# Wide attention: one reciprocal per four steps, spread to rows by DMA, multiplied by GpSimd a pass later; the output of two head pairs accumulates in PSUM

## The chip, the cores and the metric

The kernel runs on one core of one Trainium2 chip. The metric is the device time of one execution, in microseconds. The median of three runs before the change is 1040.21 us (1037.43 to 1385.11). One execution was taken by the profiler, and the trace rows below are all of that one.

## The reference

Eight sublayers in a row (four attentions, four feed-forward blocks) act on x of 4 batches x 256 tokens x 128 features, each added through a tanh gate. The change touches two of them, the "wide" attentions L1 and L3: 16 heads of 64 features, 256 queries and 256 keys per batch. Apart from names, for each batch and head:

```python
q, k, v = x @ Wq, ctx @ Wk, ctx @ Wv          # 1024 wide, 16 heads of 64
# L1 (first call):  scores masked, then w = relu(scores * scale + nbias) ** 2
# L3 (second call): scores clipped to -11..11, then w = exp(scores * scale)
attn = w / w.sum(-1)                          # L1 adds 1e-32 to the sum
out  = concat_heads(attn @ v) @ Wo            # (256, 128) per batch (+ bo in L3)
```

The division by the sum is done late: the kernel multiplies the 64 x 256 result of `w @ v` by the reciprocal of the sum.

## The kernel before

Every engine has its own instruction stream, written by hand in program order, with waits on counting semaphores between the engines. There is no scheduler: the order of the calls in each engine's `body` is the order on the engine.

A wide attention (`wide_pe`, `wide_act`, `wide_pool`, `wide_dve`; call `c` is 0 for L1 and 1 for L3) makes four **passes** (`NQ`), each over four heads, that is two **head pairs**. A pass has eight **steps** g: a step is one head pair (g // 4) and one batch (g % 4). Two steps make a **slot** k = g // 2: one head pair for one half of the 1024 tokens. The first three passes ran in a hardware loop (`Fori`), the last was written out. The work of a step and who does it:

- `scores(g)`, TensorE: twelve 64-row products into PSUM banks 0-1 or 2-3, two steps ahead of their use.
- `bound(g)`, VectorE: clips or masks the 128 x 1024 scores into one of three buffers `w_p`. It waits until GpSimd has read what stood there (`ps`).
- `weights(g)`, ScalarE: Square or Exp on that buffer.
- `values(g)`, TensorE: the weights times v, into bank 4 (two steps side by side).
- `add(g)`, GpSimd: adds the two key halves into one of two buffers `w_ps`, for the sums. It waits until `denominators` has read the last contents (`dn`).

Once per slot:

- `denominators(k)`, TensorE: sums over the keys, into bank 5, each sum repeated on 32 rows (row block 32 x (2 x head + batch)).
- `reciprocal(k)`, VectorE, on 128 x 256 (in call 0 with an addition of 1e-32 ahead of it).
- `spread(k)`, TensorE: multiplies the reciprocals by a 0/1 matrix so that each of the 64 rows of a head has them, into bank 5.
- `sums(k)`, ScalarE: copies bank 4 to SBUF (`w_pv`); `normalise(k)`, VectorE: `w_pv` times bank 5, into `w_at`.
- `output(k)`, TensorE: `w_at` times Wo, into bank 6; `add(k)`, VectorE: adds bank 6 to the accumulator `xn`.
- `project(k)`, TensorE: q and k of a slot two ahead, into banks 6 and 7; `high` (ScalarE) and `low` (VectorE) split them into two fp32r parts. `wide_values` (TensorE, four tiles per pass, banks 6 and 7) and `value_tiles` (ScalarE) make v of the next pass; `wide_weights` (VectorE, once per pass) splits the next pass's weights.

Banks 6 and 7 are thus shared by `project`, `wide_values` and `output`, and bank 5 by sums and spread reciprocals. Line numbers of before that the rows use: L180 to L182 are the three products of `mm3` (`project`, `wide_values`), L678 `scores`, L691 `values`, L704 `denominators`, L711 `spread`, L719 `output`, L811 `weights`, L851 GpSimd's `add`, L867 and L869 `wide_weights`, L896 `bound` of call 1, L905 `reciprocal` of call 1, L910 `normalise`, L917 VectorE's `add`.

## Time and profile before

| | us |
|---|---|
| median of three runs | 1040.21 |
| the profiled execution | 1033.27 |
| its span | 1031.5 |
| TensorE busy | 844.6 (82% of the span) |
| VectorE busy | 749.3 (73%) |
| ScalarE busy | 446.5 (43%) |
| GpSimd busy | 164.2 (16%) |

The span is what the trace covers; the profiled execution took 1.8 us more. Shares of busy time are averages over eight different sublayers. What the change is worth is read in the two stretches of the wide attentions: the first call from 239.4 us to 397.5 us, the second from 690.9 us to 839.1 us (from the first `values` product to the end of the last `add`).

### The profile page before, as it was taken

What the parts mean: (1) busy time and instruction counts of PE and PEld (TensorE: products, weight loads), DVE (VectorE), ACT (ScalarE), POOL (GpSimd) and SP (SyncE); (2) the same over time, 40 slices, a digit from 0 to 9 for tenths busy, and PEclk for the clock granted to TensorE, in tenths of its full rate; (3) what the DMA queues carried; (4) which work ended last, traced back from release to release, by engine and by line L of the source; (5) the groups of instructions that cost most, each with busy time, mean ns of one, the idle gap of its engine ahead of it and who ended that gap; (6) DMA issues with size and microseconds to landing.
All of it is one profiled execution on the core that took longest, in us unless ns stands there. A gap on an engine that the chain in (4) does not pass through costs nothing. (4 is left out here: it accounts for less than half of the span.)

```text
span 1031.5 us, 14938 instructions
## 1 busy us (share of the span) xinstructions
PE 844.6 (82%) x5066; PEld 602.6 (58%) x5066; DVE 749.3 (73%) x1370; ACT 446.5 (43%) x662; POOL 164.2 (16%) x131
## 2 busy tenths in 40 slices
PE   2688877768889898999947888469899958999996
PEld 2555545445656567677725554346666636777774
DVE  4688765767677776588766887758768675878785
ACT  2254452114344441599912454134443423555553
POOL 1000010003122221022220000113313220111112
PEclk9699999999989997799956999679999987999998
DMA  8000000040000000000200060000000000000000
GB/s 339 1 1 0 1 1 0 0 163 1 1 0 0 0 2 1 0 1 0 83 0 1 0 260 2 0 1 1 1 0 0 1 1 1 1 0 0 0 1 21
DMA packets 1916, 22.78 MB, mean 22 GB/s; under 512 B 209, under 2 KB 209, under 8 KB 1105
## 3 DMA queue, kind: packets, MB, share of 16 engines
q1 hardware_dynamic: 1872, 22.22, 5.3%
q8 instruction: 25, 0.41, 0.2%
q14 instruction: 19, 0.15, 0.0%
HBM read 21.70 MB, written 0.52 MB: 22 GB/s over the span
## 5 line engine op out<-in xcount | busy, mean ns | idle before, releaser
L180 PE MATMUL banks<-normed_t_high,work_split 128*128 128x512 f32 x264 | 119.7, 453 | 44.6 <-DVE normed_tokens L917 15.5
L851 POOL TENSOR_TENSOR work<-work 128x512 f32<-128x512 f32 x64 | 85.9, 1344 | 234.5 <-PE banks L704 146.6
L181 PE MATMUL banks<-normed_t_low,work_split 128*128 128x512 f32 x264 | 109.1, 413 | 0.0
L182 PE MATMUL banks<-normed_t_high,work_split 128*128 128x512 f32 x264 | 108.7, 412 | 0.0
L524 DVE TENSOR_REDUCE work<-banks 128x2 f32<-128x512 f32 x128 | 84.9, 687 | 26.5 <-PE banks L359 25.9
L180 PEld LDWEIGHTS banks<-normed_t_high,work_split 128*128 128x128 f32 x264 | 52.4, 199 | 71.6 <-issue 26.2
L471 ACT ACTIVATE work<-banks 128x1024 f32<-128x1024 f32 x64 | 65.3, 1023 | 47.1 <-PE banks L374 47.1
L241 POOL TENSOR_TENSOR ln_rstd<-ln_var_eps,minus_half 128x8 f32<-128x8 f32 x10 | 17.9, 1790 | 369.7 <-DVE ln_var_eps L225 369.7
L1654 DVE TENSOR_TENSOR work<-work,banks 128x512 f32<-128x512 f32 x68 | 46.6, 687 | 38.0 <-ACT work L1543 37.5
L691 PE MATMUL banks<-work 128*64 128x256 f32 x512 | 70.5, 397 | 4.0 <-ACT work L811 4.0
L1543 ACT ACTIVATE work<-banks 128x512 f32<-128x512 f32 x68 | 40.6, 598 | 73.1 <-PE banks L182 73.1
L359 PE MATMUL banks<-work_split 128*128 128x256 f32 x256 | 60.5, 336 | 13.3 <-DVE work L524 10.3
L180 PE MATMUL banks<-work_split 128*128 128x512 f32 x148 | 64.3, 434 | 5.9 <-DVE work_split L1617 4.4
L1402 DVE TENSOR_TENSOR work_split<-work,work_split 128x512 fp32r<-128x512 f32 x64 | 50.9, 795 | 21.8 <-ACT work_split L1329 20.7
L678 PEld LDWEIGHTS banks<-work_split 64*128 64x128 f32 x768 | 50.0, 188 | 24.4 <-issue 24.0
L359 PEld LDWEIGHTS banks<-work_split 128*128 128x128 f32 x256 | 42.5, 208 | 36.9 <-DVE work L524 25.8
L678 PE MATMUL banks<-work_split 64*128 64x256 f32 x768 | 62.8, 297 | 0.0
L182 PEld LDWEIGHTS banks<-normed_t_high,work_split 128*128 128x128 f32 x264 | 52.8, 200 | 13.0
L181 PE MATMUL banks<-work_split 128*128 128x512 f32 x148 | 59.5, 402 | 0.0
L182 PE MATMUL banks<-work_split 128*128 128x512 f32 x148 | 59.4, 401 | 0.0
L181 PEld LDWEIGHTS banks<-normed_t_low,work_split 128*128 128x128 f32 x264 | 52.9, 201 | 11.0 <-issue 1.9
L892 DVE SCALAR_TENSOR_TENSOR work<-banks,score_floor,raw_b 128x1024 f32<-128x1024 f32 x32 | 40.5, 1268 | 21.1 <-PE banks L678 21.1
(247 smaller groups left out, 1804.5 us busy)
## 6 DMA issues: line engine op xcount, KB each, us to landing
raw_b<-in_wf SPq DMA_DIRECT2D x1, 6528.0 KB, 19.2
raw_a<-in_wf SPq DMA_DIRECT2D x1, 4096.0 KB, 12.0
raw_a<-in_wf SPq DMA_DIRECT2D x1, 2048.0 KB, 13.0
raw_b<-in_wb SPq DMA_DIRECT2D x1, 2048.0 KB, 17.6
raw_a<-in_wb SPq DMA_DIRECT2D x1, 2048.0 KB, 7.9
small_operands<-in_small SPq DMA_DIRECT2D x1, 1607.0 KB, 7.1
residual<-in_x SPq DMA_DIRECT2D x1, 512.0 KB, 3.7
sublayer_out_t<-in_ctx_t SPq DMA_DIRECT2D x1, 512.0 KB, 8.0
```

Of the source, the lines that this page charges most:

```text
L180: nc.tensor.matmul(o, w[0], m[0], start=start, stop=False)
L181: nc.tensor.matmul(o, w[0], m[1], start=False, stop=False)
L182: return nc.tensor.matmul(o, w[1], m[0], start=False, stop=stop)
L359: last = nc.tensor.matmul(ps[:, 6 + n % 2, (j % 2) * S:(j % 2 + 1) * S], a_y[:, t * P:(t + 1) * P], a_km[j][:, (t // 2) * S:(t // 2 + 1) * S],
L471: nc.scalar.activation(a_p[u % 2], bank(2 * (u % 2), 2), ACT.Exp, scale=float(1.0 / np.sqrt(np.float32(DH8)))).then_inc(A["p"].sem, 1)
L524: nc.vector.tensor_reduce(a_nm[:, t, j0:j0 + 2], bank(6 + n % 2).rearrange("p (j k) -> p j k", j=2), AX.X, ALU.max, negate=True).then_inc( ...
L678: last = nc.tensor.matmul(ps[:, 2 * (g % 2) + h, kb * S:(kb + 1) * S], w_k[kt][rows, keys], w_q[qt][rows, b * S:(b + 1) * S], start=n == 0 ...
L691: last = nc.tensor.matmul(ps[DH * h:DH * (h + 1), 4, (b % 2) * S:(b % 2 + 1) * S], w_v[:, 2 * b + kb, (2 * p + h) * DH:(2 * p + h + 1) * D ...
L851: nc.gpsimd.tensor_tensor(w_ps[g % 2].rearrange("p (h q) -> p h q", h=2), v[:, :, 0, :], v[:, :, 1, :], ALU.add).then_inc(W["ps"].sem, 1)
L1402: nc.vector.tensor_tensor(g_a[n % 4][1], g_af[n % 4], g_a[n % 4][0].bitcast(F32), ALU.subtract)\
L1543: nc.scalar.activation(k_sg[n % 2], bank(n % 2), ACT.Silu).then_inc(K["sg"].sem, 1)
L1654: nc.vector.tensor_tensor(k_af[n % 2], k_sg[n % 2], bank(2 + n % 2), ALU.mult).then_inc(K["a"].sem, 1)
```

## The change

1. **One reciprocal for four slots.** In the first three passes `denominators` of slot k uses a 0/1 matrix (`den_ones`, a new part of the `small` operand) that is one only in columns 8k to 8k+7 of each block of 32, and accumulates over the four slots in bank 5. After the fourth there is one `reciprocal` per pass instead of four, into `w_rec`, which now lies in the buffer `xf`.
2. **Spread by DMA.** `wide_spread`, new on SyncE's queue, issues 16 DMAs per pass (`NSP`). Each reads one row of 256 reciprocals (1 KB) and writes it to 64 partitions of a side buffer `w_rb`, 64 KB. All 16 count on one semaphore `rb`.
3. **Multiplied by GpSimd a pass later.** `sums` copies each slot to a buffer of its own (two sets of four). GpSimd's `normalise(i, k)` multiplies it in place by `w_rb`, behind its `add` of steps 3, 4, 5 and 6 of the next pass, for slots 0, 2, 1, 3. It waits for all 16 DMAs.
4. **Output of two pairs.** `output(i, h)` multiplies slots h and 2 + h of a pass and accumulates both in bank 6; VectorE's `add` comes twice a pass instead of four times. The output of pass i is made near the end of pass i + 1.
5. **The last pass** keeps one `reciprocal`, `spread` and VectorE `normalise` per slot. The output of the pass before it and its own both fall in it.
6. The loops of the four engines are written out, `value_tiles` are placed anew, and the semaphores count through without loop bases.

```diff
+        NSP = GH * GH
-        w_pv, w_at, w_rec = wf[:, 6144:6656], wf[:, 6656:7168], wf[:, 7168:7424]
-        w_den, w_ones = wf[:, 7680:7936], wf[:, 7936:7968]
+        w_side = [t[:, a:a + 4096] for t, a in ((raw_b, 8192), (raw_a, 4096))]
+        w_rb = [[s[:, 512 * k:512 * (k + 1)] for k in range(4)] for s in w_side]
+        w_pv = [[[t[:, a + 512 * k:a + 512 * (k + 1)] for k in range(4)] for t, a in ((wf, 6144), (s, 2048))]
+                for s in w_side]
+        w_rec, w_den = xf[:, 0:S], xf[:, S:2 * S]
...
+            def denominators(x):
+                i, k = x // 4, x % 4
+                at("ps", 2 * x + 2)
+                gathered = i < LAST
+                if k == 0:
+                    at("rec", i)
+                elif not gathered:
+                    at("at", k)
                 for h in range(2):
                     for b in range(2):
                         r = BLK * (2 * h + b)
-                        last = nc.tensor.matmul(ps[r:r + BLK, 5, 0:S], w_ones, w_ps[b][:, h * S:(h + 1) * S],
-                                                start=True, stop=True)
+                        last = nc.tensor.matmul(ps[r:r + BLK, 5, 0:S], col("den_ones", BLK * (k if gathered else 4), BLK),
+                                                w_ps[b][:, h * S:(h + 1) * S],
+                                                start=not gathered or k == 0, stop=not gathered or k == 3)
...
+            def output(i, h):
+                at("acc", 2 * i + h)
+                if i < LAST:
+                    at("nm", 4 * i + 2 * h + 2)
+                for p in range(2):
+                    if i == LAST:
+                        at("at", 2 * p + h + 1)
+                    wo = raw[:, i * W_B + r0 + 3 * QW + p * P:i * W_B + r0 + 3 * QW + (p + 1) * P]
+                    for t in range(4):
+                        last = nc.tensor.matmul(ps[:, 6, t * P:(t + 1) * P], w_pv[c][i % 2][2 * p + h][:, t * P:(t + 1) * P],
+                                                wo, start=p == 0 and t == 0, stop=p == 1 and t == 3)
+                last.then_inc(W["o"].sem, 1)
```

The order of TensorE's calls, and GpSimd's and SyncE's new functions:

```diff
+            def body(i):
+                ahead = i < LAST
+                for g in range(8):
+                    x = 4 * i + g // 2
+                    values(8 * i + g)
+                    if g < 6 or ahead:
+                        scores(8 * i + g + 2)
+                    if g == 0:
+                        at("va", 4 * i + 4)
+                    if g % 2 == 0 and (g < 4 or ahead):
+                        if g == 6:
+                            at("va", 4 * i + 6)
+                        project(x + 2)
+                    if g % 2 == 1:
+                        denominators(x)
+                    if g == 5 and ahead:
+                        at("el", 2 * (x + 2) + 2)
+                        wide_values(4, 6)
+                        wide_values(5, 7)
+                    if not ahead and g in (2, 4, 6):
+                        spread(g // 2 - 1)
+                    if g == (7 if ahead else 4) and i:
+                        at("el", 2 * (x + 2 if ahead else x + 1) + 2)
+                        output(i - 1, 0)
+                    if g == 7 and ahead:
+                        at("el", 2 * (x + 2) + 2)
+                        wide_values(6, 7)
+                    if g == 5 and not ahead:
+                        output(i - 1, 1)
+                if ahead:
+                    if i:
+                        output(i - 1, 1)
+                        at("acc", 2 * i)
+                    else:
+                        at("el", 2 * (4 * i + 5) + 2)
+                    wide_values(7, 6)
+                else:
+                    output(i, 0)
+                    spread(3)
+                    output(i, 1)
...
+        def wide_pool(pool, c):
+            def normalise(i, k):
+                W["rb"].wait(pool, c, 16 * NSP * (i + 1))
+                W["pvc"].wait(pool, c, 4 * i + 4)
+                v = w_pv[c][i % 2][k]
+                nc.gpsimd.tensor_tensor(v, v, w_rb[c][k], ALU.mult).then_inc(W["nm"].sem, 1)
+            for g in range(NG8):
+                add(g)
+                i, k = g // 8 - 1, {3: 0, 4: 2, 5: 1, 6: 3}.get(g % 8)
+                if i >= 0 and k is not None:
+                    normalise(i, k)
+
+        def wide_spread(sp, c):
+            for i in range(LAST):
+                W["rec"].wait(sp, c, i + 1)
+                W["nm"].wait(sp, c, 4 * i)
+                for k in range(4):
+                    for h in range(2):
+                        for b in range(2):
+                            r = BLK * (2 * h + b) + DH8 * k
+                            sp.dma_start(w_rb[c][k][DH * h:DH * (h + 1), b * S:(b + 1) * S],
+                                         w_rec[r:r + 1, :].unsqueeze(1).to_broadcast((1, DH, S))).then_inc(W["rb"].sem, 16)
```

The order of VectorE's calls:

```diff
+            def body(i):
+                ahead = i < LAST
+                for g in range(8):
+                    x = 4 * i + g // 2
+                    if g < 6 or ahead:
+                        bound(8 * i + g + 2)
+                    if g % 2 == 0 and (g < 4 or ahead):
+                        low(x + 2)
+                    if g == 3 and ahead:
+                        at("qk", 8 * i + 8)
+                        wide_weights(dve, c, i + 1, raw, r0)
+                    if ahead:
+                        if g == 7:
+                            reciprocal(i)
+                            if i:
+                                add(i - 1, 0)
+                                add(i - 1, 1)
+                    else:
+                        if g % 2 == 0 and g:
+                            normalise(g // 2 - 1)
+                        if g == 4:
+                            add(i - 1, 0)
+                        if g == 5:
+                            add(i - 1, 1)
+                        if g % 2 == 1:
+                            reciprocal(LAST + g // 2)
+                if not ahead:
+                    add(i, 0)
+                    normalise(3)
+                    add(i, 1)
```

**GpSimd**, second pass of the first call. Before, inside the loop, it holds additions alone (the register rows come from the loop's wait values):

```order
L851 TENSOR_TENSOR work<-work 128x512 [waits w_dn]
L847 REGISTER_ALU
L851 TENSOR_TENSOR work<-work 128x512 [waits w_dn,w_p]
L847 REGISTER_ALU
L849 REGISTER_ALU [waits w_p]
L851 TENSOR_TENSOR work<-work 128x512 [waits w_dn]
```

Now (L856 is the addition, L863 the multiplication; `raw_b` is the side buffer):

```order
L856 TENSOR_TENSOR work<-work 128x512 [waits w_dn,w_p] x10
L863 TENSOR_TENSOR work<-work,raw_b 128x512 [waits w_pvc,w_rb]
L856 TENSOR_TENSOR work<-work 128x512 [waits w_dn,w_p]
L863 TENSOR_TENSOR work<-work,raw_b 128x512 [waits w_pvc,w_rb]
L856 TENSOR_TENSOR work<-work 128x512 [waits w_dn,w_p]
L863 TENSOR_TENSOR work<-work,raw_b 128x512 [waits w_pvc,w_rb]
L856 TENSOR_TENSOR work<-work 128x512 [waits w_dn,w_p]
L863 TENSOR_TENSOR work<-work,raw_b 128x512 [waits w_pvc,w_rb]
L856 TENSOR_TENSOR work<-work 128x512 [waits w_dn,w_p] x5
```

Four multiplications, each behind a wait for the DMAs, now stand in the queue ahead of additions.

**TensorE**, the last pass of the first call from the sums of slot 2 on, before (L704 sums, L719 output, L691 values, L711 spread):

```order
L704 MATMUL banks<-work 32x256 [waits w_ps,w_at]
L704 MATMUL banks<-work 32x256 x3
L719 MATMUL banks<-raw_b,work 128x128 [waits w_at,w_acc]
L719 MATMUL banks<-raw_b,work 128x128 x3
L691 MATMUL banks<-work 64x256 [waits w_pvc,w_p]
L691 MATMUL banks<-work 64x256 x3
L711 MATMUL banks<-work,small_operands 128x256 [waits w_rec]
L711 MATMUL banks<-work,small_operands 128x256
L691 MATMUL banks<-work 64x256 [waits w_p]
L691 MATMUL banks<-work 64x256 x3
L704 MATMUL banks<-work 32x256 [waits w_ps,w_at]
L704 MATMUL banks<-work 32x256 x3
```

Now (L718 sums, L740 output, L699 values, L726 spread):

```order
L718 MATMUL banks<-work,small_operands 32x256 [waits w_at,w_ps]
L718 MATMUL banks<-work,small_operands 32x256 x3
L740 MATMUL banks<-raw_b,work 128x128 [waits w_nm,w_acc]
L740 MATMUL banks<-raw_b,work 128x128 x7
L699 MATMUL banks<-work 64x256 [waits w_pvc,w_va,w_p]
L699 MATMUL banks<-work 64x256 x3
L726 MATMUL banks<-normed_t,small_operands 128x256 [waits w_rec]
L726 MATMUL banks<-normed_t,small_operands 128x256
L699 MATMUL banks<-work 64x256 [waits w_va,w_p]
L699 MATMUL banks<-work 64x256 x3
L718 MATMUL banks<-work,small_operands 32x256 [waits w_at,w_ps]
L718 MATMUL banks<-work,small_operands 32x256 x3
```

Behind the sums of slot 2 stands an output of eight products instead of four, and it waits for GpSimd's multiplications (`w_nm`).

**VectorE**, the same place, before (L902 and L903 `reciprocal`, L917 `add`, L910 `normalise`, L892 `bound`):

```order
L910 TENSOR_TENSOR work<-work,banks 128x512 [waits w_pvc,w_rb]
L892 SCALAR_TENSOR_TENSOR work<-banks,score_floor,raw_b 128x1024 [waits w_ps,w_s]
L874 REGISTER_ALU
L902 TENSOR_SCALAR work<-banks 128x256 [waits w_dn]
L99 REGISTER_ALU
L903 RECIPROCAL work<-work 128x256 [waits vector_own_steps]
L917 TENSOR_TENSOR normed_tokens<-normed_tokens,banks 128x512 [waits w_acc,w_o]
L910 TENSOR_TENSOR work<-work,banks 128x512 [waits w_pvc,w_rb]
```

Now (L926 and L927 `reciprocal`, L941 `add`, L935 `normalise`, L912 `bound`):

```order
L935 TENSOR_TENSOR raw_b<-raw_b,banks 128x512 [waits w_pvc,w_sp]
L941 TENSOR_TENSOR normed_tokens<-normed_tokens,banks 128x512 [waits w_acc,w_o]
L912 SCALAR_TENSOR_TENSOR work<-banks,score_floor,raw_b 128x1024 [waits w_ps,w_s]
L941 TENSOR_TENSOR normed_tokens<-normed_tokens,banks 128x512 [waits w_acc,w_o]
L926 TENSOR_SCALAR normed_t<-banks 128x256 [waits w_sp,w_dn]
L927 RECIPROCAL normed_t<-normed_t 128x256 [waits vector_own_steps]
L935 TENSOR_TENSOR raw_b<-raw_b,banks 128x512 [waits w_pvc,w_sp]
```

The `reciprocal` of slot 2 now stands behind the `add` of the other pass's output.

## Rows read from the trace of the kernel before

**Rows 1.** Windows: both calls, one pass of the second, two of the first.

```profile
core 0: us, PE busy (x) PEld busy (x) DVE busy (x) ACT busy (x) POOL busy (x), PEclk, DMA share, GB/s
239.40:397.50 158.10, 139.99 (x1101) 96.61 (x1102) 114.56 (x128) 66.76 (x87) 42.71 (x32) 0.96 0.00 1
690.90:839.10 148.20, 134.60 (x1092) 92.92 (x1092) 107.22 (x112) 63.78 (x87) 43.19 (x32) 0.99 0.00 1
697.70:736.30 38.60, 35.14 (x292) 24.69 (x288) 28.57 (x32) 17.36 (x24) 11.00 (x9) 1.00 0.00 1
248.20:288.30 40.10, 35.21 (x292) 24.77 (x292) 30.40 (x35) 18.22 (x25) 10.89 (x9) 1.00 0.00 1
288.30:331.30 43.00, 38.10 (x292) 26.37 (x290) 30.46 (x35) 18.14 (x25) 10.84 (x9) 0.92 0.00 0
```

**Rows 2.** Timeline of TensorE, second call: start us, length us, work, idle before it.

```profile
698.86 0.51 PE L180 MATMUL banks<-normed_t_high,work_split 128*128 128x512 f32 x1
...
700.37 1.02 PE L711 MATMUL banks<-work,small_operands 128*128 128x256 f32 x4
701.32 1.08 PE L691 MATMUL banks<-work 128*64 128x256 f32 x8
702.34 0.97 PE L678 MATMUL banks<-work_split 64*128 64x256 f32 x12
703.24 0.64 PE L704 MATMUL banks<-work 128*32 128x256 f32 x8
703.80 1.16 PE L719 MATMUL banks<-raw_a,work 128*128 x8
704.89 1.08 PE L691 MATMUL banks<-work 128*64 128x256 f32 x8
...
709.01 0.49 PE L180 MATMUL banks<-normed_t_high,work_split 128*128 128x512 f32 x1 [2.12 <-DVE normed_tokens L917]
...
725.76 0.39 PE L180 MATMUL banks<-work_split,context_t_high 128*128 128x256 f32 x1 [1.17 <-DVE normed_tokens L917]
...
726.57 1.02 PE L711 MATMUL banks<-work,small_operands 128*128 128x256 f32 x4
```

**Rows 3.** Groups by line and form, 697.7 to 736.3 us.

```profile
L905 DVE RECIPROCAL work<-banks 128x256 f32<-128x256 f32 x5 | 8.7, 1748 | 0.0
L896 DVE TENSOR_SCALAR work<-banks 128x1024 f32<-128x1024 f32 x9 | 10.9, 1216 | 6.2 <-PE banks L678 6.1
L811 ACT ACTIVATE work<-work 128x1024 f32<-128x1024 f32 x8 | 8.4, 1053 | 4.2 <-DVE work L896 4.2
L910 DVE TENSOR_TENSOR work<-work,banks 128x512 f32<-128x512 f32 x4 | 2.7, 679 | 1.9 <-PE banks L711 1.9
L917 DVE TENSOR_TENSOR normed_tokens<-normed_tokens,banks 128x512 f32<-128x512 f32 x4 | 2.6, 642 | 1.3 <-PE banks L719 1.3
```

**Rows 4.** Timeline of VectorE, first call: the split of the next weights.

```profile
294.60 1.12 DVE L867 CAST work_split<-raw_b 128x768 fp32r x1
295.76 0.96 DVE L869 TENSOR_TENSOR work_split<-raw_b,work_split 128x768 fp32r<-128x768 f32 x1
```

**Rows 5.** Line L851, both calls: min/median/max ns.

```profile
L851 POOL TENSOR_TENSOR work<-work x64: 1266/1278/2052, 239.4 to 829.6; 128x512 f32<-128x512 f32 x64
```

**Rows 6.** Timeline of TensorE, second call: sums of the last pass's slot 2.

```profile
827.09 0.64 PE L704 MATMUL banks<-work 128*32 128x256 f32 x8
```

**Rows 7.** SyncE's issues, last two of nine in a row; queue; issues with us to landing.

```profile
4.27 0.46 SPq L1702 DMA_DIRECT2D context_tokens<-in_ctx_tok  x1
4.77 0.49 SPq L1702 DMA_DIRECT2D raw_b<-in_wa  x1
...
q1 hardware_dynamic: 1872, 22.22, 5.3%
...
raw_b<-in_wf SPq DMA_DIRECT2D x1, 6528.0 KB, 19.2
...
out_tokens<-residual SPq DMA_DIRECT2D x1, 512.0 KB, 2.6
```

More of the change, by code:

```diff
@@ new lines, in wide_pe, with wide_act, at, high @@
+            pe.wait_ge(s_xs, 2 * splits(m) + 2)
+            project(0)
+            project(1)
+            at("va", 2)
+            scores(0)
+            at("va", 4)
+            scores(1)
+            for i in range(NQ):
+                body(i)
+        def wide_act(act, c, func, bias):
+            def at(name, n):
+                W[name].wait(act, c, n)
+            def high(x):
+                h = x % 2
+                at("s", 2 * x - 2)
+                at("qk", 2 * x + 1)
+                nc.scalar.activation(half(w_q[0], h), bank(6), ACT.Copy).then_inc(W["eh"].sem, 1)
+                at("qk", 2 * x + 2)
+                nc.scalar.activation(half(w_k[0], h), bank(7), ACT.Copy).then_inc(W["eh"].sem, 1)
+            def sums(x):
+                at("pv", 2 * x + 2)
+                at("o", 2 * (x // 4 - 2) + x % 2 + 1)
+                nc.scalar.activation(w_pv[c][x // 4 % 2][x % 4], bank(4), ACT.Copy).then_inc(W["pvc"].sem, 1)
+            def value_tiles(n, k):
+                m = n % 4
+                if n >= 4:
+                    at("pv", 8 * (n // 4 - 1) + 5 + m)
+                at("vp", n + 1)
+                nc.scalar.activation(w_v[:, 2 * m:2 * m + 2, :].rearrange("p t c -> p (t c)"),
+                                     bank(k), ACT.Copy).then_inc(W["va"].sem, 1)
+            def weights(g):
+                at("y", g + 1)
+                p = w_p[g % 3]
+                nc.scalar.activation(p, p, func, bias=bias, scale=0.125).then_inc(W["p"].sem, 1)
+            def body(i):
+                ahead = i < LAST
+                for g in range(8):
+                    x = 4 * i + g // 2
+                    if g % 2:
+                        sums(x)
+                    elif g < 4 or ahead:
+                        high(x + 2)
+                    if g < 6 or ahead:
+                        weights(8 * i + g + 2)
+                    if ahead and g == 5:
+                        value_tiles(4 * i + 4, 6)
+                        value_tiles(4 * i + 5, 7)
+                if ahead:
+                    value_tiles(4 * i + 6, 7)
+                    value_tiles(4 * i + 7, 6)
+            for n in range(4):
+                value_tiles(n, n)
+            high(0)
+            high(1)
+            weights(0)
+            weights(1)
+            for i in range(NQ):
+                body(i)
@@ L851, in add @@
+        def wide_pool(pool, c):
+            def add(g):
+                W["p"].wait(pool, c, g + 1)
+                W["dn"].wait(pool, c, g // 2)
+                v = w_p[g % 3].rearrange("p (h k q) -> p h k q", h=2, k=2)
                 nc.gpsimd.tensor_tensor(w_ps[g % 2].rearrange("p (h q) -> p h q", h=2), v[:, :, 0, :],
                                         v[:, :, 1, :], ALU.add).then_inc(W["ps"].sem, 1)
-            def body(i, ahead):
-                for g in range(2, 10 if ahead else 8):
-                    add(i, g)
@@ L938, in wide_dve, with body @@
[L938 to L947 removed]
+            def body(i):
+                ahead = i < LAST
+                for g in range(8):
+                    x = 4 * i + g // 2
+                    if g < 6 or ahead:
+                        bound(8 * i + g + 2)
[3 more added lines that the diff above has]
+                        at("qk", 8 * i + 8)
+                        wide_weights(dve, c, i + 1, raw, r0)
+                    if ahead:
[17 more added lines that the diff above has]
+                    add(i, 1)
@@ L949, in tokens_in @@
+            low(0)
+            low(1)
+            bound(0)
+            bound(1)
+            for i in range(NQ):
+                body(i)
         def tokens_in(dve, order, n, src):
```

287 lines of the change are left out of this document (71 added, 216 removed).

## Prediction

> **What bounds the kernel now.** I read the windows first, since busy shares of the whole span mix eight sublayers. In both wide calls TensorE is busy for nearly nine tenths of the time (139.99 of 158.10 us, 134.60 of 148.20 us), VectorE for about seven, ScalarE and GpSimd far less [rows 1]. So a pass lasts as long as TensorE's own work plus the waits that reach it. In a pass of the second call these are 35.14 us of work and 3.5 us of idle time in 38.60 us; in the first call, at the full granted clock, 35.21 us and 4.9 us in 40.10 us [rows 1]. The timeline of TensorE shows what the work is, from start to start, and who causes the idle time: `project` and `wide_values` wait for VectorE's L917, which must clear bank 6 [rows 2]. VectorE is late there because a `reciprocal` of 1.75 us stands in its queue ahead of it [rows 3].
>
> **Prices of TensorE's pieces** [rows 2]: `values` 1.02 (701.32 to 702.34), `scores` 0.90, `denominators` 0.56, `output` of a slot 1.09, `project` 1.51 (698.86 to 700.37), `spread` 0.95, one value tile 0.81 (725.76 to 726.57). A pass of before is 8 x 1.92 + 4 x 1.51 + 4 x 0.56 + 4 x 0.95 + 4 x 1.09 + 4 x 0.81 = 35.0 us, which is the 35.14 of the window. The list is complete.
>
> **The change, part by part.**
>
> *Spread leaves TensorE* in three of four passes: 4 x 0.95 = 3.8 us per pass. Accumulated sums and outputs have as many products as before, so their price is taken as unchanged. No output lies in pass 0, and the last pass has two passes' worth.
>
> *VectorE* loses three reciprocals (5.2 us), four normalisations (2.7 us) and two additions (1.3 us) per pass [rows 3]. From 28.57 us it falls to about 19.3 us; it is no bound, and this is worth only what its lateness cost TensorE. What is late next, by the new order of calls:
> - `wide_weights` (1.12 + 0.96 us [rows 4]) stands behind `bound` of step 5. `project` of step 4 needs it. Counted from the end of `scores(5)`: `bound` ends at 1.4, the split at 3.5. TensorE comes there after sums, values and scores, 2.5 us. Stall 1.1 us in each of the three gathered passes. Before, a wait for L917 covered it.
> - At the end of passes 1 and 2 bank 6 is passed on: output, `add`, output, `add`, value tile. From the end of the last `scores`: the first output ends at 0.56 + 2.18 = 2.7, a value tile at 3.5, while VectorE has `bound` (1.22) and `reciprocal` (1.75) ahead of an `add` of 0.64 [rows 3], done at 4.1. Stall 0.6, in the first call 1.0 for its extra addition. The second `add` stalls the last value tile by 0.8 more. Together 1.4 and 1.8 us.
>
> So pass 0 is 15.4 + 6.0 + 2.2 + 3.2 + 1.1 = 28.0 us, and passes 1 and 2 are 28.0 + 4.4 + 1.4 (1.8) = 33.8 us (34.2).
>
> *The last pass.* Up to the sums of slot 2: six steps 11.5, two projections 3.0, three sums 1.7, two spreads 1.9, one doubled output 2.2, a wait of 0.4 for the second `spread` = 20.7 us. Then a new chain, in us from there: GpSimd's `add` and its last multiplication come first, 2 x 1.28 [rows 5], to 2.8; output to 5.0; `add` to 5.8; only then the reciprocal, since it stands behind that `add`, to 7.55; spread to 8.6; normalise 0.68 [rows 3] to 9.4; sums to 10.0; reciprocal to 11.8; spread to 12.9; normalise to 13.7; output to 16.0; `add` to 16.7. The same stretch of before is 839.1 - 827.65 = 11.45 us [rows 1, 6]. The last pass is 37.4 us, in the first call 38.5 for its two extra additions. Before it was about 31 us: here the change loses 6 to 7 us a call.
>
> *Sum.* Second call 28.0 + 2 x 33.8 + 37.4 = 133.0 against 148.2: 15.2 less. First call 28.0 + 2 x 34.2 + 38.5 = 134.9 against 158.1: 23.2 less. Together 38.4 us.
>
> *Clock.* The first call was granted 0.96, the second 0.99 [rows 1]. At 2.4 GHz falling to 1.2 GHz, 0.96 means that 8% of 158.1 us, 12.6 us, passed at the lower level, which cost 6.3 us, and the second call lost 1.5. My pieces are priced at the upper level. Some drops follow idle time that stays elsewhere (the stalls above); I take half of the 7.8 us back: 34.5 us. Ends: 30.6 and 38.4.
>
> *GpSimd* gets 12 instructions a pass instead of 8. At 1.28 us that is 15 us, and at the longest 2.05 us [rows 5] 25 us, still below 31. It is no bound by itself. But its queue is now where the DMAs are waited for.
>
> *The 16 DMAs.* No DMA of before reads a row of SBUF 64 times, so this is the unknown. Issues follow each other at 0.50 us [rows 7]: the last leaves 7.5 us after the reciprocal, and the shortest landing in the trace is 2.6 us (512 KB). Lower end of the latency L, from reciprocal to the last landing: 10.1 us. The data, 16 x 64 KB = 1.05 MB, take 3.0 us at the rate of the 6528 KB load (19.2 us). If the reads of one row come no faster than one DMA engine moves data, they take longer: the queue moved 22.22 MB in 5.3% of 16 x 1031.5 us, 25.4 GB/s an engine [rows 7], so 2.6 us a copy, 41 us one after another. Upper end of L: 41 + 2.6 = 44 us. With ends that far apart and nothing in the trace nearer to one of them, I take the middle of the two in ratio, 11.1 us of data: L = 0.5 + 11.1 + 2.6 = 14.2 us.
>
> *When L hurts.* The additions of steps 4 and 5 stand behind the first two multiplications, and `denominators` of slot 2 waits for them: 4 x 1.3 = 5.2 us on GpSimd after the last landing. From reciprocal 0 (it ends 3.6 us after the last `scores` of pass 0) to the moment that TensorE wants those sums (20.5 us after the same point) there are 16.9 us, so L may be 11.7 us. In passes 2 and 3 the outputs at the seam give more time: 17.9 and 17.0 us. Cost of both calls: 2 x [(L - 11.7) + (L - 17.9) + (L - 17.0)], each bracket only if positive. For 14.2 us that is 5 us; for 20 us, 27; for 25 us, 57; for 44 us, 171.
>
> **The forecast.** 1033.3 - 34.5 + 5.0 = 1003.8 us for the profiled execution, which lies 6.9 us under the median of the runs; against the median, 1010 us.
>
> Here a rule bears on the choice. The Trainium skill, SBUF — State Buffer, "Door 1: The DMA port swizzle (why `[64,N]` ≈ `[32,N]`)", says that DMA reaches SBUF through 16 ports of eight partitions each, 27.2 GB/s a port, and that rows 32 apart share one. By that rule each copy takes 2.4 us at its port and the sixteen source rows lie on eight ports, so L is from about 13 us with all ports at work to over 40 us with one. No row of this case shows a port.
>
> **Rivals.**
> - *The copies queue at their source.* Place: GpSimd's first multiplication of each pass; behind it additions, then sums, then all of TensorE. For it speaks that a copy's 64 reads are all of one row, and that the next copy is issued after 0.5 us, long before 2.6 us are over. Against it, that the rows differ from copy to copy. It decides against the change from L = 21 us on (cost 34 us), and by over 2% from L = 25 us. One after another: 1040 - 34.5 + 171 = 1177 us; three copies at once (L = 17) 1016 us, two at once (L = 24) 1055 us.
> - *The waits move instead of going.* VectorE has slack now, but TensorE's queue has new waits at the seams. If idle time per pass stays as it was (3.5 and 4.9 us instead of 2.5 and 2.9), and the clock gives nothing back, 9 to 14 us of the gain go: 1019 to 1024 us with L = 14.
> - *Copies hidden and clock full:* 1040.2 - 38.4 = 1002 us, or less if the landing is short of all limits and the stalls of 1.1 us don't come (six of them, 6.6 us): 995 us.
> - *The written-out loops* cost instruction fetch, which the loop did not need. [...]
>
> **How the numbers follow.** The likeliest case, L up to 17.8 us (up to there the gain is over 2%): 0.47, with 995 to 1019 us and 1010 in its middle. L from there to 25: 0.20, 1019 to 1062. L above 25: 0.21, 1062 to 1177. Waits that move, or fetch: 0.12, 1015 to 1035. A measurement of this kernel tells about 2%, 21 us, from no change. Faster by over 2% (below 1019): 0.47 and a small part of the fourth, less the chance that the sum itself is too high by 15 us: 0.47. Slower: 0.21. Within: 0.32. A range of 8 in 10 reaches from 995 to 1065: it leaves out most of the slow case and little below.
>
> **What would show it.** Right: TensorE's pass 1 and 2 about 34 us and pass 0 28 us; GpSimd's multiplication waiting for a DMA for a few us in the second pass only; `project` waiting 1 us for L890; the tail 17 us long. Wrong: long waits of GpSimd for DMAs in every pass, the last landing over 20 us behind its reciprocal, a clock that drops in the stalls; or landings at 10 us and a gain of 35 us or more.

## The result and the profile after

The changed kernel takes 1077.95 us (median of 4 runs, 1075.87 to 1081.07), the kernel before 1038.82 us in the same comparison: ratio 1.042 (95%: 1.037 to 1.046). The ratio is taken from fast runs alone, and so without the slow one of 1385.11 us among the four of before; the two medians alone give 1.038. It is 4% slower, where 3% faster was predicted, and lies above the range. The profiled execution took 1075.87 us.

The page of the changed kernel: busy times, granted clock of TensorE in tenths over 40 slices, the queue that SyncE fills, and its new copies (KB each, median us from issue to landing).

```profile
PE 829.2 (77%) x4970; PEld 587.6 (55%) x4970; DVE 691.6 (64%) x1303; ACT 445.0 (41%) x662; POOL 189.7 (18%) x153
...
PEclk9699989999888967899957998589698796999999
...
q1 hardware_dynamic: 9552, 28.60, 14.8%
...
raw_b<-normed_t SPq DMA_DIRECT2D x48, 64.0 KB, 5.7
raw_a<-normed_t SPq DMA_DIRECT2D x48, 64.0 KB, 5.7
```

TensorE has 15 us less to do than before and VectorE 58 us less, and still the span grew by 43 us: the time is idle time of these engines. Where it lies, the windows tell: the first call from its first `values` to the end of reciprocal 0, of reciprocal 1, of reciprocal 2, and to its end; then the whole call, and the whole second call.

```profile
core 0: us, PE busy (x) PEld busy (x) DVE busy (x) ACT busy (x) POOL busy (x), PEclk, DMA share, GB/s
239.40:269.10 29.70, 28.60 (x254) 18.63 (x256) 19.69 (x21) 18.60 (x26) 13.14 (x10) 1.00 0.00 1
269.10:313.80 44.70, 29.84 (x242) 19.67 (x238) 19.04 (x21) 16.84 (x24) 15.06 (x13) 0.81 0.41 25
313.80:358.00 44.20, 34.32 (x272) 23.25 (x272) 20.18 (x23) 17.83 (x25) 14.94 (x13) 0.88 0.38 24
358.00:418.00 60.00, 40.41 (x291) 28.50 (x291) 24.91 (x29) 12.59 (x16) 12.98 (x11) 0.80 0.29 18
239.40:418.00 178.60, 133.18 (x1053) 90.05 (x1053) 83.82 (x91) 65.86 (x88) 56.13 (x44) 0.86 0.30 19
707.50:881.80 174.30, 129.56 (x1044) 87.22 (x1044) 80.44 (x84) 62.98 (x88) 55.36 (x44) 0.87 0.30 19
```

Against the whole calls in [rows 1] the first is 20.5 us longer and the second 26.1 us, together 46.6; the change of the span is all in them. Pass 0 is short and at the full clock. Each later window holds 10 to 20 us in which TensorE does nothing, and the clock that was 0.96 and 0.99 is 0.86 and 0.87.

What TensorE waits for is in the timelines of VectorE and GpSimd in the first call (start, length, work, idle time before it and what ended it). The rows are the three reciprocals of the gathered passes, and the first multiplication behind each:

```profile
267.33 1.75 DVE L927 RECIPROCAL normed_t<-normed_t 128x256 f32<-128x256 f32 x1
...
312.01 1.75 DVE L927 RECIPROCAL normed_t<-normed_t 128x256 f32<-128x256 f32 x1
...
356.28 1.75 DVE L927 RECIPROCAL normed_t<-normed_t 128x256 f32<-128x256 f32 x1
...
294.95 1.26 POOL L863 TENSOR_TENSOR work<-work,raw_b 128x512 f32<-128x512 f32 x1 [17.85 <-DMA raw_b<-normed_t]
...
339.10 1.26 POOL L863 TENSOR_TENSOR raw_b<-raw_b 128x512 f32<-128x512 f32 x1 [11.60 <-DMA raw_b<-normed_t]
...
382.93 1.27 POOL L863 TENSOR_TENSOR work<-work,raw_b 128x512 f32<-128x512 f32 x1 [11.19 <-DMA raw_b<-normed_t]
```

The reciprocals end at 269.08, 313.76 and 358.03 us, so L, from there to the last landing (taken as the start of the multiplication that waits for it), is 25.9, 25.3 and 24.9 us; in the second call 25.6, 25.7 and 25.3. TensorE and VectorE in the first call, behind those three:

```profile
299.93 0.65 PE L718 MATMUL banks<-work,small_operands 128*32 128x256 f32 x4 [14.27 <-POOL work L856]
...
344.08 1.08 PE L718 MATMUL banks<-work,small_operands 128*32 128x256 f32 x8 [8.02 <-POOL work L856]
...
382.96 0.42 DVE L926 TENSOR_SCALAR normed_t<-banks 128x256 f32<-128x256 f32 x1 [13.78 <-DMA raw_b<-normed_t]
...
385.22 2.07 PE L726 MATMUL banks<-normed_t,small_operands 128*128 128x256 f32 x4 [13.28 <-DVE normed_t L927]
```

In the gathered passes it is the chain that the prediction described: `denominators` (L718) waits for GpSimd's `add` (L856), which is queued behind the multiplication (L863). In the last pass it is another: the first reciprocal of that pass overwrites `w_rec`, and so VectorE waits until the 16 copies of pass 2 have read it. TensorE's `spread` (L726) waits for VectorE.

The clock falls in the stalls. Three windows around the first: before it, its first part, its second part.

```profile
283.00:287.00 4.00, 2.66 (x24) 1.51 (x22) 1.54 (x3) 2.72 (x4) 0.00 (x0) 1.00 0.72 58
287.00:290.00 3.00, 0.00 (x0) 0.00 (x0) 0.00 (x0) 0.00 (x0) 0.00 (x0) 0.82 0.81 49
290.00:293.00 3.00, 0.00 (x0) 0.00 (x0) 0.00 (x0) 0.00 (x0) 0.00 (x0) 0.50 0.78 41
```

In the second and third window no compute engine works, the 16 DMA engines are busy for four fifths of the time with 49 and 41 GB/s, and TensorE goes from 2.4 to 1.2 GHz. The `spread` behind the third stall took 2.07 us instead of 1.1.

### The profile page after: what moved, and what is told of

It reads as the page before. It is cut to its first block and busy times, and to the rows that moved or that the text cites. A ratio compares the mean times of both kernels' runs of the same rounds, so it can differ in the third digit from the quotient of the medians.

```text
span 1074.1 us, 14441 instructions
## 1 busy us (share of the span) xinstructions
PE 829.2 (77%) x4970; PEld 587.6 (55%) x4970; DVE 691.6 (64%) x1303; ACT 445.0 (41%) x662; POOL 189.7 (18%) x153
## 2 busy tenths in 40 slices
DMA packets 9606, 29.32 MB, mean 27 GB/s; under 512 B 1744, under 2 KB 7888, under 8 KB 8784
## 3 DMA queue, kind: packets, MB, share of 16 engines
q1 hardware_dynamic: 9552, 28.60, 14.8%
## 5 line engine op out<-in xcount | busy, mean ns | idle before, releaser
L856 POOL TENSOR_TENSOR work<-work 128x512 f32<-128x512 f32 x64 | 82.5, 1290 | 164.6 <-PE banks L718 123.5
L180 PEld LDWEIGHTS banks<-normed_t_high,work_split 128*128 128x128 f32 x264 | 51.9, 197 | 60.2 <-issue 14.7
L912 DVE SCALAR_TENSOR_TENSOR work<-banks,score_floor,raw_b 128x1024 f32<-128x1024 f32 x32 | 40.8, 1276 | 60.6 <-PE banks L687 41.9
L699 PE MATMUL banks<-work 128*64 128x256 f32 x512 | 75.9, 421 | 3.7 <-ACT work L823 3.7
L916 DVE TENSOR_SCALAR work<-banks 128x1024 f32<-128x1024 f32 x32 | 38.9, 1220 | 59.9 <-PE banks L687 41.6
L1686 DVE TENSOR_TENSOR work<-work,banks 128x512 f32<-128x512 f32 x68 | 46.6, 686 | 39.0 <-ACT work L1575 38.4
L359 PE MATMUL banks<-work_split 128*128 128x256 f32 x256 | 61.1, 341 | 12.7 <-DVE work L524 10.1
L180 PE MATMUL banks<-work_split 128*128 128x512 f32 x148 | 64.0, 433 | 5.9 <-DVE work_split L1649 4.4
L687 PEld LDWEIGHTS banks<-work_split 64*128 64x128 f32 x768 | 51.1, 192 | 25.8 <-issue 15.8
L823 ACT ACTIVATE work<-work,small_operands 128x1024 f32<-128x1024 f32 x32 | 36.7, 1148 | 53.7 <-DVE work L912 53.7
L182 PE MATMUL banks<-work_split 128*128 128x512 f32 x148 | 58.9, 398 | 0.0
```

Source lines behind the costliest of these rows:

```text
L180: nc.tensor.matmul(o, w[0], m[0], start=start, stop=False)
L182: return nc.tensor.matmul(o, w[1], m[0], start=False, stop=stop)
L359: last = nc.tensor.matmul(ps[:, 6 + n % 2, (j % 2) * S:(j % 2 + 1) * S], a_y[:, t * P:(t + 1) * P], a_km[j][:, (t // 2) * S:(t // 2 + 1) * S],
L687: last = nc.tensor.matmul(ps[:, 2 * (g % 2) + h, kb * S:(kb + 1) * S], w_k[kt][rows, keys], w_q[qt][rows, b * S:(b + 1) * S], start=n == 0 ...
L699: last = nc.tensor.matmul(ps[DH * h:DH * (h + 1), 4, (b % 2) * S:(b % 2 + 1) * S], w_v[:, 2 * b + kb, (2 * p + h) * DH:(2 * p + h + 1) * D ...
L856: nc.gpsimd.tensor_tensor(w_ps[g % 2].rearrange("p (h q) -> p h q", h=2), v[:, :, 0, :], v[:, :, 1, :], ALU.add).then_inc(W["ps"].sem, 1)
```

## The experiments

The theory after the result: the time goes only to the copies' latency L and to what waits for it. Rival: the written-out loops and the new seams cost as much by themselves. On L itself four explanations were open: a price per transfer or packet; all 64 reads being of one row; rows that lie near each other or 32 apart; the order of issue. A fifth stood in the expectations: only as many DMA engines may share a copy as it reads rows. L is given for the first pass of the first call throughout. Line numbers shift by a few where an edit adds lines.

**No copies.** The sum without L.

```diff
-            wide_spread(sp, 0)
...
-                W["rb"].wait(pool, c, 16 * NSP * (i + 1))
-                nc.gpsimd.tensor_tensor(v, v, w_rb[c][k], ALU.mult)
+                nc.gpsimd.tensor_tensor(v, v, col("sel_e", 0, HALF), ALU.mult)
```

> The changed kernel without its 96 copies and without the waits for them; GpSimd multiplies by a constant 128 x 512 tile instead of the spread reciprocals, so the normalisation of three passes is left out. Theory (the copies come back too late and everything else goes as predicted): passes of about 28, 34, 34 and 38 us, both calls together 38 us shorter than before, 997 to 1008 us by the clock. Rival (the new order of outputs, GpSimd's four extra multiplications or the written-out loops cost time by themselves): 1030 us or more, with waits of TensorE that have nothing to do with a DMA.

Measured: 1000.9 us (998.9 to 1005.73; before in this comparison 1034.25), ratio 0.968 (0.963 to 0.973). So all that the change does besides the copies is worth 33.4 us, against the 34.5 of the prediction, and the rival is out. The granted clock is 0.912, as before (0.913). The stretches between reciprocals are 29.0 and 34.7 us in the first call; in the changed kernel they are 44.7 and 44.3.

**Two buffers for the reciprocals.** The overlooked wait alone.

```diff
-        w_rec, w_den = xf[:, 0:S], xf[:, S:2 * S]
+        w_recs, w_den = (xf[:, 0:S], xf[:, 2 * S:3 * S]), xf[:, S:2 * S]
...
-                if 0 < n <= LAST:
-                    at("rb", 16 * NSP * n)
+                w_rec = w_recs[1 if n >= LAST else n % 2]
+                if 1 < n <= LAST:
+                    at("rb", 16 * NSP * (n - 1))
```

> Reciprocals of even and odd passes in two buffers, so that the last pass's first reciprocal need not wait until the copies have read the old ones. Theory (this wait is a second toll of the late copies, beside GpSimd's): additions of the last pass come 5 to 7 us earlier per call, 1062 to 1068 us against 1078. Rival (GpSimd's wait for the same copies hides it): 1076 to 1080 us.

Measured: 1063.25 us (1060.03 to 1065.97), ratio 1.027 (1.022 to 1.032) against 1.042. The wait cost 1.4% of the time, some 14 us. The two calls are 14.7 us shorter by the traces, 10.4 of it behind the third reciprocal, where the wait was. L is unchanged at 25.8 us.

**Each partition reads its own row.** The same 96 copies of 64 KB in as many packets, but from 64 rows of a constant table.

```diff
-                                         w_rec[r:r + 1, :].unsqueeze(1).to_broadcast((1, DH, S))
+                                         sm[DH * h:DH * (h + 1), SMALL["sel_e"][0]:SMALL["sel_e"][0] + S]
```

> The same 96 copies of 64 rows x 1 KB to the same places at the same moments, but each of the 64 rows is read from a row of its own (a constant table), not 64 times from one; so the multiplication is by constants. Theory A (64 reads of one row queue at it): the last landing comes at most 13 us after the reciprocal instead of 25.5, and the time falls to 1005 to 1020 us. Theory B (the DMA engines pay per 1 KB packet, wherever it is read): still 24 to 26 us and 1072 to 1082 us.

Measured: 1003.46 us (1000.29 to 1006.62), ratio 0.970 (0.964 to 0.976). L is 12.9 us. Packets and bytes are those of the changed kernel (9552, 28.60 MB), but they take 8.0% of the engines' time instead of 14.8%, and a copy lands after 2.0 us instead of 5.7. So it isn't packets, bytes, the queue or the destination; it is the source. The source is another buffer here too; the last experiment with L below reads the reciprocals themselves and rules that out.

**Eight adjacent rows, each read eight times.** The eight rows hold the same sums in the changed kernel, so the result and every wait stay as they are.

```diff
-                                         w_rec[r:r + 1, :].unsqueeze(1).to_broadcast((1, DH, S))
+                                         w_rec[r:r + DH8, :].unsqueeze(1).to_broadcast((DH8, DH8, S))
```

> Each copy reads eight rows eight times instead of one row 64 times; the eight rows hold the same reciprocals. Theory A (reads of one row queue): latency of the sixteen falls by a third or more, below 17 us, and the time to 1015 to 1040 us. Theory B (cost per packet): 25 us or more, since only as many engines can share a copy as there are rows, 1078 us or up to 1120 us.

Measured: 1024.1 us (1019.68 to 1028.53), ratio 0.990 (0.983 to 0.997), L 17.3 us, two runs. By time that is 1% under before and within the 2% that this comparison can tell. Better than one row, worse than 64.

**Another order of issue.** The same 16 copies; neighbours in the queue now read rows 8 apart and not 32 apart.

```diff
-                for k in range(4):
+                for b in range(2):
                     for h in range(2):
-                        for b in range(2):
+                        for k in range(4):
                             r = BLK * (2 * h + b) + DH8 * k
```

> The changed kernel with its sixteen copies of a pass issued in another order: slot innermost, so that copies in a row read rows 8 apart and never rows 32 apart one after the other. Nothing else changes. Theory A1 (copies in flight together wait for each other only where their source rows share a way into SBUF, and rows 32 apart do): latency falls from 25.5 to 15 to 20 us, 1020 to 1050 us. Theory A2 (each copy is limited by its own single row, and only a few copies fit in flight, whatever rows come next): 25 us and 1075 to 1080 us.

Measured: 1021.03 us (1020.08 to 1022.02; before 1038.53), ratio 0.985 (0.980 to 0.991), L 16.6 us. The landing falls from 5.7 to 4.0 us. No copy changed, only which ones are under way together. A limit per row or per copy can't explain this; a way to SBUF's rows that rows 32 apart share can. The edit parts rows 32, 64 and 96 apart all at once, and it makes four copies in a row instead of two write the same 64 partitions; which of the three distances counts wasn't tried.

**Four rows of a constant table, 16 times each: adjacent, or four apart.** Two kernels with the same number of rows, packets and bytes.

```diff
 # four adjacent
+  sm[r:r + 4, ...].unsqueeze(1).to_broadcast((4, 16, S))
 # four apart, r = BLK * (2 * h + b) + 16 * (k % 2) + k // 2
+  sm[r:r + 13:4, ...].unsqueeze(1).to_broadcast((4, 16, S))
```

> Each copy reads four adjacent rows of a constant table 16 times each (the multiplication is by constants). With the next run it tells a single row from its neighbourhood. If each row has its own limit: both alike. If four adjacent rows share one way in: this one as slow as one row, some 25 us and about 1075 us, or slower because only four engines can share a copy.

> As the run before, but the four rows of a copy are four apart. If adjacent rows share one way in, this is at least 5 us shorter in latency than the adjacent ones, and 20 us or more in time; if each row has its own limit, no difference beyond 1 us of latency.

Measured, one run each: 1142.48 us with adjacent rows, 1002.04 us with rows four apart. The line of the copies in each (ns of an issue min/median/max, first and last start), and GpSimd's first multiplication; first the kernel with adjacent rows:

```profile
L880 SPq DMA_DIRECT2D raw_b<-small_operands x48: 540/2040/2779, 270.9 to 408.4; - x48
...
307.87 1.26 POOL L863 TENSOR_TENSOR work<-work,raw_b 128x512 f32<-128x512 f32 x1 [28.96 <-DMA raw_b<-small_operands]
```

and the kernel with rows four apart:

```profile
L880 SPq DMA_DIRECT2D raw_b<-small_operands x48: 539/540/969, 269.4 to 343.5; - x48
...
282.91 1.29 POOL L863 TENSOR_TENSOR work<-work,raw_b 128x512 f32<-128x512 f32 x1 [5.52 <-DMA raw_b<-small_operands]
```

L is 37.0 and 13.5 us, and the adjacent kind is even slower than the changed kernel. Single runs carry this, but over both calls the trace gives L of 36.4 to 37.0 us six times, and the times differ by 140 us. The number of reads per row (16 in both), the number of rows, packets and bytes are the same, so what counts between these two is whether four neighbouring rows serve a copy alone. Issues show it too: 0.54 us where SyncE goes at its own pace, 2.04 us where it is held up. The first stall of the kernel with adjacent rows, as a window:

```profile
290.00:295.00 5.00, 0.00 (x0) 0.00 (x0) 0.00 (x0) 0.00 (x0) 0.00 (x0) 0.75 0.21 36
```

The DMA share is 0.21 here, where it was about 0.8 in the changed kernel.

**Eight constant rows, four apart, eight times each.**

```diff
 # r = BLK * (2 * h + b) + k
+  sm[r:r + 29:4, ...].unsqueeze(1).to_broadcast((8, 8, S))
```

> Each copy reads eight rows eight times each, as the run with eight rows did, but the rows are four apart and from the constant table. If the 17 us left there came from reads of adjacent rows: 13 us, as with 64 own rows, and 1000 to 1010 us. If they came from only eight engines sharing a copy: still 17 us and about 1024 us.

Measured, one run: 1003.78 us, L 12.1 us, an issue at 0.607 us. With 16 issues at that pace, the last leaves 9.1 us after the first; L is now that and the landing. The rival that fewer DMA engines made the eight adjacent rows slow is out: the queue has the same 8784 packets in both kernels.

**The same with the real sums.** `den_ones` puts the sums of slot k in rows k, k + 4, ..., k + 28 of each block, and each copy reads these eight rows.

```diff
-        d[k, DH8 * k:DH8 * (k + 1)] = 1
+        d[k, k::4] = 1
...
-                            r = BLK * (2 * h + b) + DH8 * k
+                            r = BLK * (2 * h + b) + k
...
-                                         w_rec[r:r + 1, :].unsqueeze(1).to_broadcast((1, DH, S))
+                                         w_rec[r:r + 29:4, :].unsqueeze(1).to_broadcast((8, 8, S))
```

> The whole computation again: slot k's sums go to rows k, k+4, ..., k+28 of each block of 32 instead of 8k to 8k+7, and each copy reads those eight rows eight times. The source rows are now four apart, as in the run with eight constant rows. Latency 12 to 13 us; 1000 to 1008 us, 3% under the kernel before. If latency stays at 17 us, the spacing was not the cause with real data, and the time is 1020 us or more.

Measured: 1002.05 us (6 runs, 999.95 to 1007.16; before 1034.72), ratio 0.968 (0.964 to 0.973). L is 12.1 us. The change as a whole is now 3.2% faster than before, by an edit in three lines. Its copies:

```profile
L880 SPq DMA_DIRECT2D raw_b<-normed_t x48: 607/607/1335, 269.3 to 345.1; - x48
```

**The tail.** On top of it, two buffers for the reciprocals, and in the last pass `output` (i-1, 1) behind `spread` of slot 2, so that `reciprocal` of slot 2 doesn't stand behind that output's `add`.

```diff
-                    if g == 5 and not ahead:
-                        output(i - 1, 1)
...
                         spread(g // 2 - 1)
+                    if g == 6 and not ahead:
+                        output(i - 1, 1)
```

> The run before, with the reciprocals of even and odd passes in two buffers, and in the last pass the second output of the pass before it (and its add) moved from behind the sums of slot 2 to behind slot 2's spread. Theory (the prediction's chain: GpSimd's multiplication, the doubled output and its add stand ahead of the reciprocal of slot 2): the reciprocal no longer waits, 3 to 5 us per call less, 993 to 999 us. Rival (the tail has enough slack elsewhere, or another wait takes over): 1000 us or more.

Measured: 998.05 us (6 runs, 993.31 to 1000.4), ratio 0.965 (0.961 to 0.969). The 4.0 us between the medians are within the spread of the runs, but the traces show where the calls get shorter. The reciprocal of slot 2 starts at 361.38 us instead of 369.04, and the first call ends 5.9 us earlier (375.45 against 381.33 us). The two edits weren't tried apart; the wait for the old reciprocals that the first one takes away was 1.5 and 0.9 us in the trace of the version before.

**The weights' split one step earlier.** The predicted stall of `project` on the split.

```diff
-                    if g == 3 and ahead:
+                    if g == 2 and ahead:
                         at("qk", 8 * i + 8)
```

> The run before, with the split of the next pass's weights one step earlier on VectorE. Theory (it costs TensorE 1.0 us in three passes of each call, as predicted and seen ahead of the projection in step 4): 4 to 6 us less, 988 to 994 us. Rival (the two VectorE instructions then delay the bounds of step 5 as much): no change.

Measured: 984.46 us (6 runs, 980.58 to 988.12), ratio 0.950 (0.946 to 0.955): the fastest kernel of the study, 5% under before, and below the 988 to 994 us expected. The pass between reciprocals 1 and 2 of the second call, first without this edit, then with it (windows as above):

```profile
725.66:761.59 35.93, 32.93 (x274) 22.21 (x273) 21.05 (x22) 17.02 (x24) 16.15 (x13) 0.95 0.09 30
```

```profile
723.93:756.24 32.31, 31.25 (x274) 21.51 (x274) 19.33 (x23) 16.92 (x24) 15.19 (x13) 1.00 0.10 34
```

3.6 us for a stall of 1.1 by the prediction. TensorE's timeline without the edit shows two parts: the wait, and slower products behind it.

```profile
742.00 1.08 PE L699 MATMUL banks<-work 128*64 128x256 f32 x8
...
745.93 0.50 PE L180 MATMUL banks<-normed_t_high,work_split 128*128 128x512 f32 x1 [1.95 <-DVE work_split L891]
...
746.91 0.63 PE L180 MATMUL banks<-context_t_high,work_split 128*128 128x512 f32 x1
...
748.32 1.85 PE L699 MATMUL banks<-work 128*64 128x256 f32 x8
```

After 1.95 us of waiting a product takes 0.63 us instead of 0.40 and `values` 1.85 instead of 1.08. The wait itself is longer than predicted because the split is: VectorE's and GpSimd's timelines of the same moment, without the edit, show why.

```profile
742.68 1.27 DVE L889 CAST work_split<-raw_a 128x768 fp32r<-128x768 f32 x1
743.98 1.90 DVE L891 TENSOR_TENSOR work_split<-raw_a,work_split 128x768 fp32r<-128x768 f32 x1
...
743.49 1.58 POOL L863 TENSOR_TENSOR raw_a<-raw_a 128x512 f32<-128x512 f32 x1
745.03 1.99 POOL L856 TENSOR_TENSOR work<-work 128x512 f32<-128x512 f32 x1
```

Beside GpSimd's instructions the split takes 1.27 + 1.90 us, and GpSimd's take 1.58 and 1.99 us instead of 1.28. One step earlier it mostly runs where GpSimd rests, and takes 0.55 + 0.96 us in all six places. Without the edit the six stalls were 1.01, 0.36 and 1.95 us in the first call and 2.09, 1.39 and 1.95 in the second, 8.8 us together; with it there are none. Only the last of them was followed by a fall of the clock.

By the traces the two calls are 3.7 and 6.4 us shorter with the edit, 10.1 together. The profiled executions differ by only 5.6 us, since the part ahead of the first call, which no edit touches, took 4.1 us more in the second trace. The medians differ by 13.6 us. The profiled execution of the version without the edit was its fastest, so single steps are uncertain; over the last two experiments together the medians fell by 17.6 us and the profiled executions by 16.5.

All kernels together, by L:

| source of a copy | packets of the queue | L, us | landing, us | time, us |
|---|---|---|---|---|
| no copies | 1872 | - | - | 1000.9 |
| 8 rows four apart, constants | 8784 | 12.1 | - | 1003.8 |
| 8 rows four apart, real data | 8784 | 12.1 | - | 1002.1 |
| 64 own rows | 9552 | 12.9 | 2.0 | 1003.5 |
| 4 rows four apart | 8400 | 13.5 | - | 1002.0 |
| 1 row, neighbours in the queue 8 apart | 9552 | 16.6 | 4.0 | 1021.0 |
| 8 adjacent rows | 8784 | 17.3 | - | 1024.1 |
| 1 row, neighbours 32 apart (the change) | 9552 | 25.9 | 5.7 | 1078.0 |
| 4 adjacent rows | 8400 | 37.0 | - | 1142.5 |

The kernel before took 1034.3 to 1038.8 us in the comparisons of these runs.

## Why the prediction was wrong, step by step

- **The failing step is the size of L.** The ends 10.1 and 44 us enclosed it, the middle in ratio, 14.2, was a guess between them, and 25.5 us came (24.9 to 25.9 in the six places). The row from which the upper end was made, 25.4 GB/s an engine [rows 7], said nothing of sources. The rule of the Trainium skill that was weighed beside it (SBUF — State Buffer, "Door 1: The DMA port swizzle (why `[64,N]` ≈ `[32,N]`)") points at what the experiments found: the four rows of a group, and the rows 32 further on, share a port. Its 27.2 GB/s a port makes an estimate of 2.4 us a copy; the kernel with four adjacent rows shows 35 us for 16, 2.2 us, which agrees within a tenth. Worked through in the order of issue it would have spoken against the change: of the four copies of each k, the first two share one port and the last two another. Two ports at a time make an estimate of 19.3 us for the 1.05 MB, and with the prediction's 0.5 and 2.6 us an L of 22.4 us, above its 21. I had only counted that the sixteen rows lie on eight ports.
- **The lower end was too low:** 12.1 us is the least L seen, with issues at 0.607 us rather than 0.50 and a landing of 2 us. Break-even against before was given as L = 21 us; that the kernel with 17.3 us was 1.0% faster and the one with 25.9 us 4.2% slower doesn't contradict it. But against the kernel without copies an L of 17.3 us costs 23 us, where the formula says 12, and a straight line from there to 25.5 us puts break-even near 19 us (an estimate).
- **The rival "the copies queue at their source" is what happened,** in place and mechanism, with a chance of 0.21. Its price was too low. By its formula L = 25.5 costs 60 us. Against the kernel without copies, the changed one loses 15.7, 9.6 and 14.8 us in the three stretches behind the reciprocals of the first call, and 14.6, 9.8 and 15.0 in the second: 79.3 us before rounding (77.1 between the medians). The formula gives 13.8, 7.6 and 8.5 a call. (For two copies at once, L = 24, it gives 1056 us and not the 1055 of the text.) The third is the overlooked wait on `w_rec`: 6.4 us more a call, 12.8 in all, and two buffers gave back some 14, 10.4 of it in this stretch. The first two are over by 3.4 us a call, where the clock fell to 0.81 and 0.88 and products behind the stalls ran at the lower level; that share wasn't isolated.
- **The clock term had the wrong sign.** Half of 7.8 us was to come back; the calls went from 0.96 and 0.99 to 0.86 and 0.87. Without copies the whole clock is as before, 0.912, and the calls have 0.98 and 0.97; worked out as in the prediction that is 6.9 us lost, so 0.9 of the 7.8 us came back instead of 3.9.
- **The sum without L was right:** 34.5 us predicted, 33.4 measured. Its pieces less so: pass 0 was 28.2 us in the first call and 30.8 in the second, from its first `values` to that of pass 1 (28.0 predicted), the stretches from reciprocal to reciprocal without copies 29.0 and 34.7 us (28.0 and 34.2), whole calls 138.5 and 136.4 us (134.9 and 133.0). The calls are 7.0 us over together, and 31.4 us under [rows 1], of the 32.0 between the profiled executions. The pieces were priced at the full clock, whose lower level cost 6.9 us here, and the stalls on the split took 3.6 us more than predicted (below): other pieces must have been some 3.5 us too dear, so part of the agreement is luck.
- **The stall of `project` on the split** was predicted as 1.1 us in each of six passes. In the changed kernel it came as 1.01, 0.36 and 0.36 us in the first call and 2.08, 0.30 and 0.30 in the second, 4.4 together; without copies as 1.0 to 2.1 us, 10.2 together. The term was mis-sized because the split hasn't one price: 0.55 + 0.96 us where GpSimd stands waiting for the copies, up to 1.27 + 2.06 us beside its instructions, against the 1.12 + 0.96 of [rows 4].
- **The last pass's tail** was right: from the end of slot 2's sums at 865.3 us to 881.8, 16.5 us, 16.7 predicted, in the second call. The version with the tail reordered shows that most of its excess over before was the order.
- **The waits that move, and the written-out loops:** without copies 1000.9 us leaves no room for either. The instruction queues carry 54 packets instead of 44. The loops were not tried alone, and no run shows a price of a loop's seam.

## What to carry to other kernels

When data leaves an engine for DMAs, the wait that decides is from the last producer to the last landing, and its price must follow every reader of the target and every writer of the source: here GpSimd's queue on one side, the next reciprocal on the other. Copies that repeat SBUF rows should each read rows four apart; if each has only one row to read, neighbours in the queue shouldn't read rows 32, 64 or 96 apart. A small stall of TensorE can cost twice its length when the clock falls behind it, as it did behind one of six here, so where a stall is cheap to move, move it. And the price of a VectorE instruction is to be read from a row in which GpSimd does what it will do in the new kernel.

## What the runs showed of the hardware

- 16 copies of 64 KB within SBUF, one queue, take from 12.1 to 37.0 us by their source rows. Reads of neighbouring rows (four or eight) get in each other's way, and so do copies of one row each whose rows are 32, 64 and 96 apart, against 8 apart (L 25.9 and 16.6); when a copy reads eight rows four apart, the last of the 16 lands about 3 us after its issue (L 12.1, issues over 9.1).
- Four adjacent rows read 16 times (L 37.0) were slower than one row read 64 times in the same order of issue (25.9). Sharing a way by rows doesn't tell these two apart. The traces show one difference: a copy of four rows has 68 packets in the queue and one of one row 80, and while TensorE stands still the DMA share is about 0.20 with 28 to 36 GB/s against about 0.80 with 41 to 49. So fewer engines work on a copy of four rows; that this makes the difference wasn't tried.
- SyncE issues such a copy in 0.46 to 0.61 us when nothing holds it, and in 1.2 to 2.0 us (median) when the source is crowded; the issue's duration in the trace is thus a sign of it.
- The queue's share of engine time rises with the crowding at the same bytes and packets (8.0% against 14.8%), so a high DMA share at 40 to 58 GB/s means waiting and not moving. A low share doesn't mean the opposite: the most crowded kernel, with four adjacent rows, has 8.4%.
- TensorE fell from 2.4 to 1.2 GHz within a stall of 14 us, and right behind one of 1.95 us. Behind stalls of 1.95 and 2.09 us in the same trace and of 2.08 us in the changed kernel's it stayed at 2.4 GHz.
- VectorE's split of weights and GpSimd's additions and multiplications slow each other: 0.96 us becomes 1.73 to 2.06, and 1.28 us becomes 1.58 to 1.99.
